# AdaLN block (attention, then a routed mixture of experts) on one core: four instruction queues in a new order from the sixth batch's attention on, the last two weight splits and six low halves moved from GpSimd to VectorE, Silu two batches earlier

## The reference, cut to what matters

```python
h = _layernorm(x) * (1 + ca) + sa
x = x + ga * _L0_attn_ref(h, ...)          # softmax(QK + cam_bias) V, then a projection
h = _layernorm(x) * (1 + cb) + sb
logits = h @ gate_weight.T                  # 8 experts
topk_w, topk_i = _group_limited_topk(softmax(logits))     # two experts for a token
e = silu(h @ gate_w.T) * (h @ up_w.T) @ down_w.T           # of each expert
shared = silu(h @ sh_gate_w.T) * (h @ sh_up_w.T) @ sh_down_w.T
x = x + gb * (routed + shared)
```

## Time and profile before

| | us |
|---|---|
| median of 3 runs | 308.44 |
| lowest and highest | 307.14, 309.18 |
| the profiled execution, its own time | 309.42 |
| its span, first to last instruction | 307.7 |

### The profile page before, as it was taken

The page is one execution under the profiler, slowest core; times in us unless marked ns, Lnnn a source line. Parts: engine busy times, 40 slices in busy tenths (PEclk is TensorE's granted clock), DMA queues, the critical chain, the costliest instruction groups (busy, mean ns, idle before and its releaser), DMA issues.

```text
span 307.7 us, 6160 instructions
## 1 busy us (share of the span) xinstructions
PE 265.2 (86%) x1801; PEld 244.3 (79%) x1801; DVE 200.4 (65%) x582; ACT 159.7 (52%) x427; POOL 138.4 (45%) x156
## 2 busy tenths in 40 slices
PE   1799999889999999799985881999999999999900
PEld 1697698879899899688884681999999999999800
DVE  2667754359987745974899780155556556867894
ACT  1538468787566746565303332255656656556500
POOL 3120416453440388577974866000544445445440
PEclk9999999999999999989998596699999999999975
DMA  7891043532231022243100235322343456684554
GB/s 233 300 334 36 0 132 107 145 108 68 68 108 37 17 106 88 69 123 124 34 17 35 72 112 201 89 53 71 113 118 117 139 168 202 196 232 141 168 189 136
DMA packets 29319, 36.98 MB, mean 120 GB/s; under 512 B 4468, under 2 KB 23903, under 8 KB 29288
## 3 DMA queue, kind: packets, MB, share of 16 engines
q1 hardware_dynamic: 24056, 27.19, 29.5%
q0 software_dynamic: 3408, 8.46, 7.7%
q10 hardware_dynamic: 1824, 0.94, 1.0%
HBM read 24.78 MB, written 12.71 MB: 122 GB/s over the span
## 4 chain that ended last, share of the span: by engine, by line
PE 75%; DVE 10%; issue 5%; ACT 3%; POOL 2%; DMA 2%; ACTq 1%; POOLq 0%; DVEq 0%
PE bank L346 18%; PE bank L348 17%; PE bank L347 16%; PE bank L1128 4%; PE bank L1365 3%; PE bank L1343 3%; PE bank L1100 3%; PE bank L1083 2%; PE bank L1111 2%; PE bank L1120 2%; PE bank L1092 2%; POOL routed_in L697 1%; PE bank L1001 1%; DMA routed_out<-yo_all,dest 1%; DMA mh<-routed_out 1%
## 5 line engine op out<-in xcount | busy, mean ns | idle before, releaser
L1431 POOL DMA_INDIRECT routed_out<-yo_all,dest x39 | 40.1, 1028 | 65.7 <-ACT yo_all L1392 51.9
L346 PE MATMUL bank<-experts_w,h2T_lo 128*128 (+1 forms) x156 | 50.8, 325 | 0.1
L347 PE MATMUL bank<-experts_w,h2T_hi 128*128 (+1 forms) x156 | 47.2, 303 | 0.0
L348 PE MATMUL bank<-experts_w,h2T_hi 128*128 (+1 forms) x156 | 47.1, 302 | 0.0
L697 POOL DMA_INDIRECT routed_in<-h2all,slot_u x32 | 31.7, 990 | 14.1 <-issue 7.6
L346 PE MATMUL bank<-h2T_hi,wsgu_lo 128*128 128x256 f32 (+1 forms) x96 | 28.9, 301 | 7.1 <-issue 6.6
L1420 DVE SCALAR_TENSOR_TENSOR wstage<-wstage,wt,bank 128x176 f32<-128x176 f32 x39 | 15.5, 397 | 29.2 <-ACT wstage L1382 29.2
L346 PEld LDWEIGHTS bank<-experts_w,h2T_lo 128*128 128x128 f32 (+1 forms) x156 | 29.5, 189 | 0.5 <-issue 0.5
L347 PEld LDWEIGHTS bank<-experts_w,h2T_hi 128*128 128x128 f32 (+1 forms) x156 | 29.6, 190 | 0.1
L348 PEld LDWEIGHTS bank<-experts_w,h2T_hi 128*128 128x128 f32 (+1 forms) x156 | 29.3, 188 | 0.0
L347 PE MATMUL bank<-h2T_lo,wsgu_hi 128*128 128x256 f32 (+1 forms) x96 | 27.6, 288 | 0.0
(11 more groups left out here) (250 smaller groups left out, 791.1 us busy)
## 6 DMA issues: line engine op xcount, KB each, us to landing
h2all<-routed_in SPq DMA_DIRECT2D x39, 130.0 KB, 2.1
wstage<-gu_t SPq DMA_DIRECT2D x8, 352.0 KB
res<-x SPq DMA_DIRECT2D x4, 512.0 KB, 8.4
mx<-modrow SPq DMA_DIRECT2D x8, 256.0 KB
mh<-modrow SPq DMA_DIRECT2D x8, 256.0 KB, 3.1
exchange<-routed_out SPq DMA_DIRECT2D x8, 256.0 KB
wmod_s<-w_mod SPq DMA_DIRECT2D x3, 512.0 KB, 9.9
wstage<-down_t SPq DMA_DIRECT2D x8, 176.0 KB
```

The lines of the kernel that those rows point to most:

```text
L346: pe.matmul(out_ap, l[1], r[0], start=start, stop=False)
L347: pe.matmul(out_ap, l[0], r[1], start=False, stop=False)
L348: return pe.matmul(out_ap, l[0], r[0], start=False, stop=stop)
L1431: pool.indirect_dma_start(out=routed_out, out_offset=bass.IndirectOffsetOnAxis(dest[:, t % 16:t % 16 + 1], 0), in_=yo[t % 6], in_offset=No ...
```

## The change

It does five things.

1. The four hand-written orders are dealt out anew from the attention of batch 5 on.
2. `lo_on_dve` takes in batches 3 and 4: six low halves move from GpSimd to VectorE. Two calls `split_weights`, of experts 6 and 7, move there too.
3. `SILU_FROM` goes from 6 to 4: six gates (q = 4, 5) take one VectorE instruction in place of two.
4. The router's scratch tiles `r_rank`, `r_pos` (in the selection) and `r_slot` move from SBUF to a PSUM bank (`MATCH`, `REST`, `SLOT`). `r_both`, the sum of the two selections, is gone: TensorE counts over both selections in turn, twice the small matmuls in `pe_rank`.
5. The expert table takes one matmul with a plain matrix of ones as weights in place of two with a broadcast column as weights.

```diff
-            return q in (5, 6, 7)
+            return q in (3, 4, 5, 6, 7)
-        SILU_FROM = 6
+        SILU_FROM = 4
-            pe.matmul(TAB[:, 0, :], ecol[:].to_broadcast([P, P]), onehot[:], start=True, stop=True)
-            pe.matmul(TAB[:, 1, :], rcol[:].to_broadcast([P, P]), onehot[:], start=True, stop=True).then_inc(s_tabmm_done, 1)
+            pe.matmul(TAB, ones[:], onehot[:], start=True, stop=True).then_inc(s_tabmm_done, 1)
...
             for j in range(NB - 1):
-                last = pe.matmul(RNK[:, (j + 1) * NE:].rearrange("p (t e) -> p t e", e=NE), ones[:],
-                                 r_both[:, j:j + 1, :].to_broadcast([P, NB - 1 - j, NE]), start=False, stop=(j == NB - 2))
+                for c in range(2):
+                    last = pe.matmul(RNK[:, (j + 1) * NE:].rearrange("p (t e) -> p t e", e=NE), ones[:],
+                                     r_sel[:, c, j:j + 1, :].to_broadcast([P, NB - 1 - j, NE]), start=False, stop=(j + c == NB - 1))
...
-            n = done(dve.tensor_tensor(r_rank[:], best, per_expert(top), ALU.is_equal))
+            n = done(dve.tensor_tensor(MATCH, best, per_expert(top), ALU.is_equal))
             dve.wait_ge(s_rt_b, n)
-            n = done(dve.scalar_tensor_tensor(r_rank[:], r_rank[:], -float(NE), eidx[:].unsqueeze(1).to_broadcast([P, NB, NE]),
+            n = done(dve.scalar_tensor_tensor(MATCH, MATCH, -float(NE), eidx[:].unsqueeze(1).to_broadcast([P, NB, NE]),
                                               ALU.mult, ALU.add))
...
-            if c == 1:
-                dve.tensor_tensor(r_both[:], r_sel[:, 0], r_sel[:, 1], ALU.add).then_inc(s_both_ready, 1)
...
                     pool_scatter(pool, 1, 5)
+                    pool_xg(pool, 7)
+                    split_weights(pool, 5)
+                    make_x1(pool, 6)
+                    make_x1(pool, 7)
                     pool_scatter(pool, 1, 6)
-                    make_x1(pool, 7)
```

More of the change, by code:

```diff
@@ L583, in pe_table @@
             pe.wait_ge(s_order_ready, 2)
-            pe.matmul(TAB[:, 0, :], ecol[:].to_broadcast([P, P]), onehot[:], start=True, stop=True)
-            pe.matmul(TAB[:, 1, :], rcol[:].to_broadcast([P, P]), onehot[:], start=True, stop=True).then_inc(s_tabmm_done, 1)
+            pe.matmul(TAB, ones[:], onehot[:], start=True, stop=True).then_inc(s_tabmm_done, 1)
         def pe_rank(pe, p):
             pe.wait_ge(s_both_ready, p + 1)
-            pe.matmul(RNK, before[:], r_both[:].rearrange("p t e -> p (t e)"), start=True, stop=False)
+            for c in range(2):
+                pe.matmul(RNK, before[:], r_sel[:, c].rearrange("p t e -> p (t e)"), start=(c == 0), stop=False)
             pe.matmul(RNK, ones[:], ebase[:].rearrange("p t e -> p (t e)"), start=False, stop=False)
@@ L602, in pe_rank @@
                 for j in range(TT):
-                    pe.matmul(CNT[:, 3:5, :], ones[:], r_both[:, j:j + 1, :].to_broadcast([P, 2, NE]), start=False, stop=False)
+                    for c in range(2):
+                        pe.matmul(CNT[:, 3:5, :], ones[:], r_sel[:, c, j:j + 1, :].to_broadcast([P, 2, NE]), start=False, stop=False)
                 for j in range(TT, NB):
-                    last = pe.matmul(CNT[:, 4, :], ones[:], r_both[:, j, :], start=False, stop=(j == NB - 1))
+                    for c in range(2):
+                        last = pe.matmul(CNT[:, 4, :], ones[:], r_sel[:, c, j, :], start=False, stop=(j + c == NB))
             last.then_inc(s_rank_done, 1)
@@ L680, in dve_slots @@
             dve.wait_ge(s_rt_c, n)
-            n = done(dve.tensor_reduce(r_slot[:], r_tmp[:], AX.X, ALU.add))
+            n = done(dve.tensor_reduce(SLOT, r_tmp[:], AX.X, ALU.add))
             dve.wait_ge(s_rt_c, n)
-            dve.tensor_copy(slot_u[:, :, p * NB:(p + 1) * NB], r_slot[:]).then_inc(s_slots_ready, 1)
+            dve.tensor_copy(slot_u[:, :, p * NB:(p + 1) * NB], SLOT).then_inc(s_slots_ready, 1)
             if p < NPAIR - 1:
-                counts = r_both[:].rearrange("p t e -> p e t")
+                counts = r_sel[:].rearrange("p c t e -> p e (c t)")
                 n = done(dve.tensor_reduce(r_sum[:], counts, AX.X, ALU.add))
@@ L2164, in _ @@
                     pe_down(pe, 3)
+                    pe_up(pe, 5, 0)
                     pe_rank(pe, 3)
-                    pe_up(pe, 5, 0)
                     pe_up(pe, 5, 1)
+                    pe_down(pe, 4)
                     pe_order(pe)
                     pe_up(pe, 5, 2)
-                    pe_down(pe, 4)
+                    pe_up(pe, 6, 0)
+                    pe_up(pe, 6, 1)
+                    pe_down(pe, 5)
+                    pe_up(pe, 6, 2)
                     pe_table(pe)
-                    pe_up(pe, 6, 0)
-                    pe_down(pe, 5)
-                    pe_up(pe, 6, 1)
-                    pe_up(pe, 6, 2)
                     pe_up(pe, 7, 0)
```

252 lines of the change are left out of this document (127 added, 125 removed).

## The result

The changed kernel takes 298.56 us in the median of 4 runs (297.87 to 299.45), the kernel before 308.1 us (307.14 to 309.18): a ratio of 0.968, 95% interval 0.964 to 0.972, faster by 3.2%. The forecast was 296.0. The profiled execution took 299.12 us (span 297.3), 10.3 us under the profiled one of before, which at 309.42 was 1.3 us over its own median.

What follows compares the result with a forecast made beforehand. Bound: TensorE idle 16.0 us and partly at low clock from 121 to 209.8 us, with VectorE, stalled by GpSimd's SBUF reads, binding at 147.8 to 165.3. Terms summed to 17.9 us (290.5); 12.4 expected: 296 us, range 288 to 305.

Steps and rivals of the forecast that it cites:

- reserve: Held back from the full sum: 3 to 4.5 us for a returning low-clock stretch, 2 us for unseen waits.
- (d): `pe_down(3)` to `pe_down(4)`, 172.36 to 185.06 us: clock gain less a new 2.3 us wait, 0.3 us, bounds -2 and +2.
- (e): 185.12 to 191.34 us: TensorE's largest wait hangs on the order and goes, 6.2 us; either 0 or 6.2.
- (a): Pair 1, 121 to 147.8 us: shorter selection and better clock, less a later root for pair 2; 2.2 us, between 0 and 3.4.
- (b): 147.8 to 165.3 us, VectorE bound: stalls beside GpSimd go, moved work comes in; 4.1 us, bounds 2 and 6.3.
- (c): 165.3 to 172.36 us, transposes to `pe_down(3)`: full clock, quicker low half, shorter selection waits; 2.0 us, 0.5 if the clock drops.
- over 0.6 us: Sign that the prediction is wrong: low halves on VectorE taking longer than 0.6 us.
- "collision" rival: Moved low halves and splits on VectorE held by GpSimd's scatters, deciding over 0.5 us each: slower, 313 us, chance 0.06.
- the wait stays: Rival: TensorE's 6.2 us wait is not a matter of order and remains, 302 us, chance 0.14.
- (f): 191.34 to 209.8 us: TensorE's lost clock, a consequence of the wait before, returns; 3.1 us, between 0 and 3.1.
- one of the two long ones comes back: Ahead of the tile phase: one of two long low-clock stretches of TensorE was expected to return, 3 to 4.5 us.
- The tiles: Scatters need 21.5 us, first tiles in by about 186, TensorE asks at about 189: covered by 3 us.

Runs made afterwards that it cites:

- e7: Kernel before with only the change's edits to selection, rank, weights and table; queue order, low halves, splits and Silu as they were: 295.03 us, ratio 0.986.
- e8: Changed kernel with the selection's three scratch rows back in SBUF: 289.61 us, ratio 0.968 to the kernel before.
- e6: Changed kernel with all eight pad register reads ahead of the eight pad copies, not held back: 288.36 us, ratio 0.962 to the kernel before.
- e4: Kernel before with SyncE's pad copies held until GpSimd's scatters have landed, nothing else: 308.8 us, ratio 1.031 to the kernel before.
- e5: Changed kernel, pad reads ahead, pad copies held until the scatters landed, first four tiles' rows read ahead: 293.93 us, ratio 0.984 to the kernel before.
- e1: Changed kernel with SyncE's eight pad copies held until all of GpSimd's scatters have landed: 299.8 us, ratio 1.002 to the kernel before.

## Why the prediction was right, and where it was not

The range held and the sign and size of the gain were right, but the total of 296.0 against 298.56 hides a step that failed and a reserve that nearly paid for it. Up to the end of (d) the sum had 8.6 us; the marks give 9.9, of which 0.4 was there at 74 us already. From there to the tile phase it had 6.2 + 3.1 - 5.5 = 3.8 us; the marks give 0.1. That the measured time still lies in the range is in part luck: the 5.5 us were held back for the clock and for waits that I did not see, not for a wrong (e).

- **(a), (b), (c): right.** Forecast 2.2 + 4.1 + 2.0 = 8.3 us up to `pe_down(3)`; behind the early mark the marks give 3.4, 8.0 - 3.8 = 4.2, and 10.1 - 8.0 = 2.1. (a) came out at its upper bound of 3.4: the clock stayed up (1.00 instead of 0.94), and the root of pair 2, of which I had feared that it eats the gain, cost VectorE one wait of 0.89 us. (b) and (c) are the terms as put. No selection instruction is over 0.3 us. The leftover of the port is one low half of 0.95 instead of 0.42 us, at 160.40 beside GpSimd's addition. That is the sign of being wrong "over 0.6 us" and a hold of the size with which the "collision" rival decides (0.5 us), but one of ten and not ten.
- **Why (a) and (b) work** was only half seen. I gave both to the shorter instructions. For (a) that holds by and large: e7 has 2.9 of the 3.4 us with the routing part alone. For (b) e7 shows that in the old order the stall moves to the next SBUF instruction (1.3 us), and e8 that in the new order it hardly occurs even with SBUF scratch (4.1 us).
- **(d): the sum about right, the new wait mis-sized.** The marks give -0.2 for 0.3 us. I had a wait of 2.3 us ahead of `pe_down(4)`. In e6, where nothing else disturbs, it is 0.56 us, and `pe_down(4)` begins 5.0 us behind the end of `pe_down(3)` instead of the 6.0 of my chain. In the changed kernel it begins 6.5 us behind, and TensorE lost the time earlier: 1.52 us ahead of `pe_up(5, 0)`, for a copy of batch 3's result that itself began 0.9 us late, and the pauses of 0.51 and 0.45 us in `pe_up(5, 1)`. The table load was on the path as said, but two roundings ran back to back (0.71 us for both) and the low halves came in VectorE's gaps. ScalarE's timeline of the changed kernel settles the price of the load too:

```profile
165.57 0.60 ACT L477 ACTIVATE og<-bank 128x512 f32<-128x512 f32 x1 [1.56 <-PE bank L345]
166.19 1.28 ACT L435 ACT_TABLE_LOAD   x1
167.48 0.38 ACT L435 ACTIVATE sact<-bank 96x256 f32<-96x256 f32 x1
167.76 0.71 ACT L443 ACTIVATE aT_hi<-aact 128x256 fp32r<-128x256 f32 x2
```

- The copy ends at 166.17, the load begins at 166.19 and the Silu at 167.48: 1.28 us and nothing around it. The 1.4 us more that the Trainium skill would charge for draining ("ScalarE: Activation LUTs", "What ACT_TABLE_LOAD costs") are not there; keeping to the row was right.
- **(e): this step failed.** "I take the wait to hang on this order and to go." It did not go: the changed kernel waits 6.49 us, behind `pe_up(5, 2)` instead of `pe_down(4)`. It goes with the chip, or with what else went with its group of runs, and not with the order: on A and B no traced kernel has it, in the old order (e4, e7) or the new, and the kernel before is faster by 8.4 to 8.7 us without any edit; on the chip of the result and on C every traced kernel has it, in either order. The 6.2 us were not the change's to win, and the rival "the wait stays", at 0.14, had this step right. Its cause stays open.
- **The clock, (f):** the 3.1 us hung on (e) and did not come. TensorE ran at the lower level from 184.5 to 190.0 behind its wait, as before from 191.3 to 197.5. Of three low stretches this one stayed, behind the wait, as the text said with "one of the two long ones comes back". 23.8 us at the lower level became 10.3.
- **The tiles** were in time where the pads run beside the scatters: in e6 the pads begin at 175.0 and TensorE never waits for a tile, in e5 and e1, with the last pad issued at 183.5 and 190.1, it waits 3.9 and 9.0. I had counted the scatters but not the pads behind them, 8.45 us if they were ever to come last.

What the change is worth where nothing is late follows from chip B alone: between 9.8 us (e8, its weaker form) and 11.1 (e6, with the reads ahead), 3.2 to 3.8%, much as on the chip of the result, where both kernels carry the wait. That the changed kernel itself has none on chip B is inferred from its relatives, and so is its gain there.

## What to carry to other kernels

A wait that the profile gives to nobody ("issue", "remote"), behind matmuls that had long ended, is no gain to put in a forecast. The word alone says little (VectorE's 5.65 us before 115 us are "issue" in the changed kernel's trace and "ACT h2T_hi" in that of e6), the late end does: run the unchanged kernel on a second chip before building on it, and never compare two versions that did not run beside the same reference. When an engine's small instructions are stretched by another engine's SBUF work, taking an operand out of SBUF can be most of the cure (pair 1, 2.9 of 3.4 us), or only pass the stall on to the next instruction that uses the port (pair 2, 1.3 of 4.2 us, with GpSimd at work for 5 us on end); there it was moving the work apart that helped (4.1 us). And when a transfer is held back to cure something, add up all that is queued behind it: here eight pad copies, 8.45 us, became the new bound at once.

## What was unexpected of the hardware

- The kernel before takes 299.4 and 299.7 us on two chips, 307.4 on a third and 308.1 on the chip of the result, which may be that third. The traces at hand with the slower times all show ends of TensorE's work that other engines see up to 7.5 us late, between 168 and 191 us, beside GpSimd's scatters.
- A copy of four elements a partition, SBUF to SBUF, was held for 5.32 us, through five GpSimd instructions in a row (e7).
- Reading a row number into a register and checking it costs SyncE about as much as issuing the copy: 1.06 us in turn, 0.5 us with the reads ahead, eight times over.
- VectorE's writes to PSUM cost it nothing to speak of: 199 ns against 191 for the same instruction.
